# Cross-attention on one core: scores three entries ahead, the row maximum as rows of the query stack, group work in three places

## The reference

```python
q = (Q @ Wq.T).reshape(B, S, H, Dk).transpose(0, 2, 1, 3)
k = (K @ Wk.T).reshape(B, S, H, Dk).transpose(0, 2, 1, 3)
v = (V @ Wv.T).reshape(B, S, H, Dk).transpose(0, 2, 1, 3)
scores = jnp.einsum('bhqd,bhkd->bhqk', q, k) / jnp.sqrt(jnp.float32(Dk))
attn = jax.nn.softmax(scores, axis=-1)
ctx = jnp.einsum('bhqk,bhkd->bhqd', attn, v)
ctx = ctx.transpose(0, 2, 1, 3).reshape(B, S, E)
return ctx @ Wo.T
...
x = x + _L0_xattn_ref(_layernorm(x, axis=-1), ctx_1024, ctx_1024, mask_1_bf0, L0_xattn_Wq, L0_xattn_Wk, L0_xattn_Wv, L0_xattn_Wo)
```

## Time and profile before

| what | us |
| --- | --- |
| median of 3 runs | 1870.25 (1869.73 to 1874.83) |
| the profiled execution | 1893.17 |
| its span | 1891.4 |
| PE busy | 1498.1 (79%) |
| DVE busy | 1068.1 (56%) |
| ACT busy | 778.0 (41%) |
| POOL busy | 462.3 (24%) |
| first ACT copy of A_outT to the last: A0, A1, A2 | 50.1 to 260.2, 815.0 to 1042.5, 1136.0 to 1372.1 |

### The profile page before, as it was taken

One profiled execution on the slowest core, in us unless ns is written; L12 is line 12 of the kernel. 1 busy time (PEld: TensorE's weight loads), 2 busy tenths in 40 slices (PEclk: granted clock), 3 DMA queues, 4 the chain that ended last, 5 costly groups with the idle time before them and its releaser, 6 DMA issues. The chain is left out here.

```text
span 1891.4 us, 43279 instructions
## 1 busy us (share of the span) xinstructions
PE 1498.1 (79%) x14594; PEld 1225.4 (65%) x14607; DVE 1068.1 (56%) x3418; ACT 778.0 (41%) x1494; POOL 462.3 (24%) x546
## 2 busy tenths in 40 slices
PE   3899967999999999689999769779979965139910
PEld 1777756988889898367777327567757655139910
DVE  2677754434443434488888557558867767313322
ACT  1566633444444444245555435446623352014400
POOL 2233321101100001122222222223312123740066
PEclk9999987999999999689999869889989996569955
DMA  5765510000000000245543023232120031112222
GB/s 155 193 179 153 155 62 1 1 1 0 0 1 0 1 0 0 76 129 128 147 117 85 1 61 109 68 92 81 53 112 0 5 123 45 52 53 93 93 70 75
DMA packets 102114, 130.94 MB, mean 69 GB/s; under 512 B 10478, under 2 KB 82434, under 8 KB 95536
## 3 DMA queue, kind: packets, MB, share of 16 engines
q1 hardware_dynamic: 97912, 121.54, 22.9%
q0 software_dynamic: 4096, 8.07, 1.5%
HBM read 88.13 MB, written 41.77 MB: 69 GB/s over the span
## 5 line engine op out<-in xcount | busy, mean ns | idle before, releaser
L475 DVE TENSOR_REDUCE A_neg_max<-A_s_bank 128x4 f32<-128x512 f32 x408 | 272.2, 685 | 123.3 <-PE A_s_bank L570 115.1
L357 ACT ACTIVATE A_probsT<-A_st_bank 128x512 f32<-128x512 f32 x384 | 227.8, 599 | 114.1 <-PE A_st_bank L585 107.7
L583 PE MATMUL A_st_bank<-A_q_stack,A_k_stack 72*128 72x128 bf16 x1536 | 225.4, 224 | 23.2 <-issue 22.1
L1759 PEld LDWEIGHTS E_y_bank<-E_w,E_h 128*128 128x128 f32 x2048 | 237.8, 192 | 5.3
L1759 PE MATMUL E_y_bank<-E_w,E_h 128*128 128x128 f32 x2048 | 239.7, 275 | 0.0
L1656 ACT ACTIVATE E_h<-E_h_bank,w_L_b 128x512 f32<-128x512 f32 x260 | 173.0, 691 | 160.2 <-PE E_h_bank L1749 158.1
L585 PE MATMUL A_st_bank<-A_max_partsT,pick_head 96*128 96x128 bf16 x1536 | 224.9, 223 | 0.0
L583 PEld LDWEIGHTS A_st_bank<-A_q_stack,A_k_stack 72*128 72x128 bf16 x1536 | 156.3, 103 | 51.2 <-issue 49.5
L570 PE MATMUL A_s_bank<-A_k_stack,A_q_stack 72*128 72x128 bf16 x1632 | 166.2, 227 | 28.7 <-DVE A_neg_max L475 23.3
L1585 DVE SCALAR_TENSOR_TENSOR x_sb<-E_y_bank,E_gates,x_sb 128x128 f32 x256 | 72.0, 344 | 181.1 <-PE E_y_bank L1759 180.3
L585 PEld LDWEIGHTS A_st_bank<-A_max_partsT,pick_head 96*128 96x128 bf16 x1536 | 153.6, 100 | 12.2 <-issue 10.6
(11 more groups left out here) (270 smaller groups left out, 3054.5 us busy)
## 6 DMA issues: line engine op xcount, KB each, us to landing
A_q_stack<-q_scratch SPq DMA_DIRECT2D x51, 576.0 KB
A_k_stack<-k_scratch SPq DMA_DIRECT2D x34, 576.0 KB
q_scratch<-A_q_parts SPq DMA_DIRECT2D x54, 192.0 KB, 2.3
A_ctxT<-in_ctxT SPq DMA_DIRECT2D x39, 256.0 KB, 6.4
k_scratch<-A_k_parts SPq DMA_DIRECT2D x36, 192.0 KB
q_scratch<-A_q_parts SPq DMA_DIRECT2D x54, 128.0 KB, 2.2
slots_in<-F_zeros SPq DMA_DIRECT2D x10, 512.0 KB, 5.0
E_xe<-slots_in SPq DMA_DIRECT2D x40, 128.0 KB, 2.2
```

Of the source, the lines that this page charges most:

```text
L357: act.activation(probsT[n % 2][:, c * HQ:(c + 1) * HQ, :], st_bank[c % 2][:, :].rearrange("k (a q) -> k a q", a=HQ), ACT.Exp, scale=scale) ...
L475: dve.tensor_reduce(neg_max[:, c * HQ:(c + 1) * HQ], s_bank[c % 2][:, :].rearrange("q (a k) -> q a k", a=HQ), AX.X, ALU.max, negate=True). ...
L583: pe.matmul(dst, k_stack[slot][:, h % kheads, at:at + S], q_stack[slot][:, h, at:at + S], start=True, stop=False)
L1759: last = pe.matmul(y_bank[e % 2][:, j * D:(j + 1) * D], h[e % 2][:, f, j * S:(j + 1) * S], w2[:, e, f, :], start=(f == 0), stop=(f == FC - 1))
```

## The change

- The stacks get three more rows (WITH_MAX = COMBO + 3). In k_stack they are ones, written once by POOL at the stage's start; in q_stack they are the three parts of the negated maximum. `scoresT` then makes one product of 75 rows per head instead of two; pick_head, its load and its cast are gone. `scores` uses the first 72 rows.
- The parts come into q_stack by a DMA that ACT issues in `copy_max`, after it has waited for its own copy; scoresT waits for max_loaded. max_parts is packed (columns 0, 16, 32).
- Scores, row_max and split_max run three entries ahead (two before); entry 2 is scored ahead of the loop. `copy_max` of entry b + 2 stands behind exps 1 in ACT's order, `transpose_max(b + 2)` behind the first block of scores in PE's. Before: entry b + 1, behind exps 2 and behind scoresT 2.
- A group has twelve places, three per entry; the third is at the entry's end. In A0 and A2: V 0, K1 1, X 2, Q1 3; in A1: V 0, K1 1, K2 2, X 3, Q1 4, Q2 5. Statistics at 9 and normalise at 11, both one group further ahead (before 0 and 2); those of group 2 come ahead of the loop.
- SP loads both halves of the stacks of group NG, where it had loaded one.

```diff
+WITH_MAX = COMBO + 3
...
-        PLACE = {V: 0, K1: 1, X: 3, Q1: 4}
+        PLACE = {V: 0, K1: 1, X: 2, Q1: 3}
     U = V + 1
-    STATISTICS, NORMALISE = 0, 2
+    PLACES = 3
+    STATISTICS, NORMALISE = 9, 11
...
+                    if isinstance(g, int) and g == 0 and half == 0 and step == 0:
+                        sp.wait_ge(ones_done, 4)
...
-                for half in range(1 if isinstance(g, int) and g == NG else 2):
+                for half in range(2):
...
+            for n, t in enumerate(k_stack):
+                pool.memset(t[64:WITH_MAX, :, :], 1.0).then_inc(ones_done, 1)
+                pool.wait_ge(ones_done, n + 1)
...
             inverse_deviation(0)
             inverse_deviation(1)
+            inverse_deviation(2)
...
-                    inverse_deviation(it * 2 + gg + 2)
                     split_rest(pool, own, k_f, k_parts, kd, it * 2 + gg + 2, KL, k_lead, k_split)
                     split_rest(pool, own, q_f, q_parts, D, it * 2 + gg + 2, QL, q_lead, q_split)
+                    inverse_deviation(it * 2 + gg + 3)
...
-                act.copy(max_partsT[q][:, :], wo_bank16[0:96, 0:S]).then_inc(mt_copied, 1)
+                act.copy(max_partsT[q % 2][:, :], wo_bank16[0:96, 0:S]).then_inc(mt_copied, 1)
+                act.wait_ge(mt_copied, b + 1)
+                at = (q % 2) * S
+                act.dma_start(q_stack[q // 2 % 4][COMBO:WITH_MAX, :, at:at + S],
+                              max_partsT[q % 2][0:3 * NH, :])\
+                    .then_inc(max_loaded[q % 2], 16)
...
                     exps(b, n, 1)
+                    copy_max(b + 2, n + 2)
                     place(0)
                     exps(b, n, 2)
-                    copy_max(b + 1, (n + 1) % 2)
                     copy_out(b)
                     exps(b, n, 3)
                     place(1)
+                    place(2)
...
+            statistics(2)
+            normalise(2, 2)
+            for b in range(3):
...
                     add_x(b)
-                    split_max(b + 2)
+                    split_max(b + 3)
                     place(1)
+                    place(2)
...
-                    pe.wait_ge(mt_copied, b + 1)
+                    pe.wait_ge(max_loaded[n % 2], PIECES * (4 * scores.it + n // 2 + 1))
...
-                    pe.matmul(dst, k_stack[slot][:, h % kheads, at:at + S], q_stack[slot][:, h, at:at + S],
-                              start=True, stop=False)
-                    last = pe.matmul(dst, core.pick_head[:, h, :], max_partsT[n % 2][:, :], start=False, stop=True)
+                    last = pe.matmul(st_bank[c % 2][:, a * S:(a + 1) * S], k_stack[slot][:, h % kheads, at:at + S],
+                                     q_stack[slot][:, h, at:at + S], start=True, stop=True)
...
                     scoresT(b, n, 0)
-                    scores(b + 2, n + 2, 0)
+                    scores(b + 3, n + 3, 0)
+                    transpose_max(b + 2)
                     scoresT(b, n, 1)
                     transpose_outT(b)
...
                     scoresT(b, n, 2)
-                    transpose_max(b + 1)
-                    scores(b + 2, n + 2, 2)
+                    scores(b + 3, n + 3, 2)
```

More of the change, by code:

```diff
@@ L121, in sem @@
             return sems[-1]
-        q_stack = [sb(f"q_stack{i}", [COMBO, NH, HALF], BF16) for i in range(4)]
-        k_stack = [sb(f"k_stack{i}", [COMBO, kheads, HALF], BF16) for i in range(4)]
+        q_stack = [sb(f"q_stack{i}", [WITH_MAX, NH, HALF], BF16) for i in range(4)]
+        k_stack = [sb(f"k_stack{i}", [WITH_MAX, kheads, HALF], BF16) for i in range(4)]
         ctxT = [sb(f"ctxT{i}", [D, GT], F32) for i in range(2)]
@@ L161, in multi_head_attention @@
         mt_copied = sem("mt_copied")
+        max_loaded = [sem(f"max_loaded{i}") for i in range(2)]
+        ones_done = sem("ones_done")
         st_ready = sem("st_ready")
@@ L416, in _ @@
                     place(1)
+                    place(2)
             copy_outT(NB)
             copy_out(NB)
+            for loaded in max_loaded:
+                act.wait_ge(loaded, PIECES * (NB // 2 + 1))
         @block.vector
@@ L521, in _ @@
                         split_rest(dve, own, q_f, q_parts, D, g, QL, q_lead, q_split)
-            for b in range(2):
+            statistics(2)
+            normalise(2, 2)
+            for b in range(3):
                 for c in range(4):
@@ L540, in place @@
                             prep(use, g, (n // GB + (1 if use == V else 2)) % 2)
-                    row_max(b + 2, 0)
-                    row_max(b + 2, 1)
+                    row_max(b + 3, 0)
+                    row_max(b + 3, 1)
                     divide(b)
@@ L569, in scores @@
                     h = c * HQ + a
-                    last = pe.matmul(s_bank[c % 2][:, a * S:(a + 1) * S], q_stack[slot][:, h, at:at + S],
-                                     k_stack[slot][:, h % kheads, at:at + S], start=True, stop=True)
+                    last = pe.matmul(s_bank[c % 2][:, a * S:(a + 1) * S], q_stack[slot][0:COMBO, h, at:at + S],
+                                     k_stack[slot][0:COMBO, h % kheads, at:at + S], start=True, stop=True)
                 last.then_inc(s_ready, 1)
@@ L656, in _ @@
             transpose_max(0)
+            for c in range(4):
+                scores(2, 2, c)
+            transpose_max(1)
             with loop_of(pe) as it:
@@ L679, in _ @@
                     scoresT(b, n, 3)
-                    scores(b + 2, n + 2, 3)
+                    scores(b + 3, n + 3, 3)
                     place(1)
@@ L2286, in load_rest @@
                 sp.dma_start(dst, src).then_inc(rest_loaded, 16)
-        with nc.sbuf_tensor("wide_pick", [96, NH, S], F32) as wide_pick, nc.Block() as block:
-            first_loads.append((wide_pick[:, :, :], ap["pick_head"], "wide_pick"))
+        with nc.Block() as block:
             @block.sync
@@ L2312, in _ @@
                 dve.tensor_copy(core.ident16[:, :], core.ident[:, :])
-                dve.tensor_copy(core.pick_head[:, :, :], wide_pick[:, :, :])
         def convert_rest():
@@ L2357, in shape_constants @@
     c = {"ident": np.eye(128, dtype=np.float32)}
-    pick = np.zeros((96, 16, 128), np.float32)
-    for part in range(3):
-        for h in range(16):
-            pick[32 * part + h, h, :] = 1.0
-    c["pick_head"] = pick
     c["iota8"] = np.arange(8, dtype=np.float32).reshape(1, 8)
```

34 lines of the change are left out of this document (19 added, 15 removed).

## The result

| what | before | after |
| --- | --- | --- |
| median, us | 1872.54 (1869.73 to 1883.47, 4 runs) | 2015.92 (2004.71 to 2019.41, 4 runs) |
| profiled span, us | 1891.4 | 2011.8 |
| to the first copy of A_outT | 50.1 | 64.8 |
| A0, first copy to last | 210.1 | 242.4 |
| E0 and A1's start | 554.8 | 591.4 |

The ratio is 1.0744, with a 95% interval of 1.0681 to 1.0806. The side was forecast (slower, 0.76), the size was not: +143 us against +29, far outside the range of 1860 to 1925. The profiles differ by 120 only, because that of before holds two code stalls, waits of PE for its own instructions, which not all of its executions seem to have (e7).

What follows compares the result with a forecast made beforehand. The prediction took PE to bound the attention loops, the second DVE as well, all chained with little slack on PE. Terms 0 + 11 + 0 + 23.6 + 11.3 - 26.6 + 10 = +29.3 gave 1900 us, range 1860 to 1925.

Steps and rivals of the forecast that it cites:

- Removed products: scoresT: 1,536 fewer products, 88 us of PE issue, a gain if PE stays the bound, nothing if another chain is as long.
- The chain in the loops: Attention loops: PE's 0.91 us an entry becomes waiting; 0 us in first and third, +11 us in second.
- DMA by ACT: copy_max: issue of 0.43 us, 0.55 an entry with the wait, covered on ACT; cost 0.
- Ones: Stage starts: four POOL memsets, 14.3 us by elements, delay first rstd; +9.3 first attention, +14.3 second, 0 third; +23.6 together.
- Third entry ahead: Ahead of the loops: extra row_max and split; +2.9 us in first and third attention, +5.5 in second, +11.3 together.
- PE's code: Instruction fetch: third attention's two stalls of 13.3 us go, -26.6; first expert loop touches eight packets and stalls, +10.
- the wait on issue: Sign: PE waits 3 to 4 us for instructions at the head of the first expert loop's second turn.
- rival (c): Third attention's stalls are in the profiled execution alone, so nothing is given back or refetched; 1916 us, chance 0.15.
- Rival (a): Attention loops: PE stays the bound, split ready in time; 1856 us if half is felt, 1812 if all; chance 0.17.
- the waits at transpose_max: Sign: in the attention loops PE idles at transpose_max, released by DVE's split step.
- the packets: Sign: no nine packets in a third-attention turn, but some eight in the first expert loop's second turn.
- The groups of 25, 30 and 26 us: Sign: group times forecast for the first, second and third attention loops.

Runs made afterwards that it cites:

- E0: Not a run: the expert loop stage of the first ffn, between first and second attention; with the second attention's start 554.8 us before, 591.4 after.
- e7: Kernel before with 40 semaphore increments on PE ahead of the third attention's first wait, shifting its loop's code; ratio 0.9947 to the kernel before.
- e3: Kernel before with the pick_head product left out of scoresT, so the maximum is not added; ratio 0.9977 to the kernel before.
- e11: e3 with each scoresT product issued twice in the second attention alone; ratio 0.9917 to the kernel before.
- e2: Changed kernel with the group's places as before, early transpose kept; ratio 1.0657 to the kernel before, 2002 us.
- e4: Kernel before with only the early transpose of the next entry's maximum and its copy behind exps 1; ratio 1.0307 to the kernel before.
- e6: Changed kernel with each 75-row product in scoresT issued twice; no ratio, loops 255, 272 and 254 us.
- e9: Changed kernel without the three rows, their ACT DMA and the ones, so the maximum is not added; ratio 1.0559 to the kernel before.
- e5: Changed kernel with transpose, copy, places, statistics and normalise in the old order, except second-attention queries one place sooner; ratio 1.0446 to the kernel before, 1976 us.
- e10: e5 and e9 together: changed kernel with the order undone and without the three rows; ratio 1.0137 to the kernel before.
- e12: Changed kernel with the ones written two at a time as 32-bit words; ratio 1.0667 to the kernel before.
- e8: Changed kernel with 170 semaphore increments on PE at the first attention's start, shifting the expert loop's code; ratio 1.0686 to the kernel before.
- e1: Changed kernel with transpose_max back behind the third block of transposed scores and its copy behind exps 2; ratio 1.0667 to the kernel before.
- e13: e5 with the early transpose kept: changed kernel with old places, statistics and normalise; ratio 1.0509 to the kernel before.

## Why the prediction was right or wrong, step by step

1. *Removed products.* Right that they would not be felt, for the reason given: another chain is as long. e3 puts them at 10 us in A0 and 1 in A2. What the step missed is their other side: in A1 their absence costs 12 us through the clock, of which e11 gives back 9.

2. *The chain in the loops*, 0, +11 and 0 us. **Here the prediction failed.** Measured: +32, +25 and +29 (A2 against e7). Three things were in it.
   - The entries. At the full clock a group takes 26.80, against the 23.95 written out. The first entry was put at 8.3 and takes 9.0 to 10.1 at the full clock: X at the entry's end waits for K's copies, and on ACT the copy of A_outT then waits behind X's (226.02, then 226.50). e2 gives this back.
   - The held steps of DVE. They were seen and set aside as the same 1.4 us before and after. That was the wrong sentence. Before, the transpose stood three blocks later and covered them. After, PE waits for them, some 1.4 us in the third entry of each group of A0 and 1.24 in A2. Without low clock that makes A2's third entry 5.96, put at 4.75. A cost that both kernels have on one engine counts anew where the other engine's wait has moved. e4 shows it with nothing else changed.
   - The clock, which the sum did not hold at all, although had 0.83 in one window. Groups of the same work in A2 go from 26.8 (1.00) to 30.7 (0.83, 10 us low) and 30.9 (0.77, 14 us low), so a low microsecond costs 0.3 to 0.4. With some 189 low us more in the three loops (A2 against e7) this is an estimated 55 to 75 us of their 86. A2 by itself agrees: at the full clock its group is 1.0 us longer than before, 8 us in the loop, and the other 21 of its 29 go with 70 low us. The waits cause the low stretches (e4: work unchanged, A1's go from 3 to 41 us), and so does missing work (e3). More work does not bring the clock back in A0 and A2; in A1 it does, as far as e6 can tell.
   In A1 the mechanism named, that K2 and Q2 wait for DVE's first half, is what the waits show, 28 us for 16 waits; it was put at 1.2 us each and is 1.7.

3. *DMA by ACT.* The issue is 0.73 us on ACT's queue; the 0.43 was read on SP's. That it costs next to nothing in the new order is right (0.15 us an entry at the full clock, and e9's loops are no shorter in sum). In the old order it costs 10 us in A0 and 20 in A2 (e5 against e10). So the early transpose pays for something; the prediction had not said for what.

4. *Ones*, by elements, 14.3 and +23.6. Right: 14.19 us for four, 14.25 later in A1. Without rows (e9) the first copy comes 14 us sooner in A0 and 16 in A1. e12 measures the rule itself. The Trainium skill, "VectorE: DVE Perf Modes", section "Zero memsets can be issued as uint32 (trn2)", had it for VectorE and zero; the runs show it on POOL, with ones.

5. *Third entry ahead*, +11.3. Mis-sized. With step 4's terms taken out (9.3 and 14.3), A0's start keeps 5.4 for 2.9, A1's 10.3 for 5.5 and A2's 4.8 for 2.9; by e9, which has no ones, A1's is 8.2 and A2's 3.8. Besides, PE waits for q_stack's load in A0's second group, which no step had.

6. *PE's code*, -26.6 and +10. The count of the blocks fits what e7 and e8 show. A2's stalls are gone, and E0's turns take 2.1, 4.1 and 3.6 us more, with about 2 in the first. But the wait on issue near a turn's head is 1.48, 1.91 and 1.53 us, not 3 to 4; the second and third of these turns also have 3 us each at 1.2 GHz. And -26.6 exists in the profile only in part of the executions: rival (c) was half right, which is why the medians lie 143 apart and the profiles 120. The Trainium skill, "Runtime: NRT & Kernel Launch", section "Instruction fetch mechanics", gives PE room for 2,048 instructions in blocks of 256, and a stall at a branch whose target is out of the current two-page window. The traces agree with neither bound: turns of loops that touch seven blocks brought no packets after the first (E0 in e8, A2 in e7), and turns of those that touch eight brought up to nine.

Rival (a) is refuted by the waits at transpose_max, and e3 shows that even without them next to nothing of the 88 us would be felt. Of the signs named, the memsets, A1's start, the waits at transpose_max and the packets came as told, the wait on issue at half its size. The groups of 25, 30 and 26 us did not come: they are 29 to 33, 29 to 32 and 27 to 33.

What stays open: the part of each wait in the low stretches, since e1, e2 and e13 each moved them from one entry to another; and whether the kernel with e12, a cheap code shift and a lighter first entry could reach the kernel before. The one that does beat both here and computes the same is e7.

## What to carry to other kernels

Before removing work from an engine, measure the ceiling: leave the work out and add nothing. One run (e3) would have shown that 88 us of products were worth 2 to 4. And when a wait is moved to an earlier place, ask what its releaser does at worst, not on average: here a held DVE step of 1 us, covered before, came out in nearly each group, and in many it came out twice on PE, as the wait and as the lower clock behind it.

## What the runs showed of the hardware

- In a loop that is otherwise busy a wait of 1.41 us was followed by some 7 us at 1.2 GHz (234.17 and 237.50). Not each is: behind one of 1.40 us, at 155.52 in A0, the clock was 1.00 from 155.6 to 170.6. Stretches at 1.2 GHz brought the mean clock down to 0.84 to 0.91 in loops whose PE is still busy for 80 to 85% of the time.
- Issuing more products can make a loop faster: 512 more took A1 from 239.7 to 230.8 us (e3, e11).
- Issuing a DMA of 12 KB takes 0.73 us of ACT's queue.
- Code stalls come in some turns of a loop and not in others (A2's packets, e7). They seem to come in some executions and not in others too: 28 us between the kernel's runs, 6 with the code shifted by 40 instructions.
